# Adapter rows loaded during stage 0, staged tiles asked for one weight group later, and the adapter sums' mask moved to ScalarE

## The reference, cut to what is computed

```python
# layer 0: a dense layer plus a signed one, scaled per batch item
x = x + (x @ W.T + b + (x @ (2 * mask[b] - 1)) * coeff[b])
# layer 1: gated feed-forward (F = 2752), each product with a rank-16 adapter chosen per batch item
def lora_add(base, inp, A, B):
    t = einsum('bri,bni->bnr', A[idx], inp)
    return base + einsum('bor,bnr->bno', B[idx], t) * 0.5
gate = lora_add(x @ W_gate.T, x, A_gate, B_gate)
up   = lora_add(x @ W_up.T,   x, A_up,   B_up)
act  = silu(gate) * up
x = x + lora_add(act @ W_down.T, act, A_down, B_down)
```

## Time and profile before

| | us |
|---|---|
| median of three runs (1623.53 to 1625.01) | 1624.55 |
| the profiled execution, its own time | 1624.44 |
| its span, first to last instruction | 1622.4 |
| TensorE busy | 1562.2 |
| VectorE busy | 1223.7 |
| ScalarE busy | 795.9 |
| POOL busy | 355.1 |
| mean granted TensorE clock | 0.993 |

### The profile page before, as it was taken

How to read it: one execution, slowest core, us unless ns; L and a number is a source line. 1 busy time by engine, 2 the same in 40 slices (tenths; PEclk the granted TensorE clock), 3 DMA queues, 4 the chain that set the end, 5 groups by cost and what they waited for, 6 DMA issues and landing times. The chain is left out here.

```text
span 1622.4 us, 23032 instructions
## 1 busy us (share of the span) xinstructions
PE 1562.2 (96%) x7508; PEld 1309.9 (81%) x7508; DVE 1223.7 (75%) x2150; ACT 795.9 (49%) x1478; POOL 355.1 (22%) x677
## 2 busy tenths in 40 slices
PE   6999978999999999999999979999999999999999
PEld 6999956888888888878887757888888888778887
DVE  7998858666667667688887797666666666788886
ACT  7998835444444444443333454444444444433332
POOL 0100021222222222253420012212222222442100
PEclk9999989999999999999999999999999999999999
DMA  8979653444444444698592723444444444996653
GB/s 327 354 285 332 230 166 91 147 147 153 153 153 153 152 136 138 215 358 271 184 372 93 256 73 118 152 148 143 136 145 153 153 153 142 333 346 207 228 198 120
DMA packets 135046, 316.85 MB, mean 195 GB/s; under 512 B 19856, under 2 KB 43536, under 8 KB 134928
## 3 DMA queue, kind: packets, MB, share of 16 engines
q0 software_dynamic: 56608, 175.81, 32.8%
q1 hardware_dynamic: 73712, 131.18, 24.1%
q10 hardware_dynamic: 4608, 8.39, 1.4%
HBM read 225.13 MB, written 90.18 MB: 194 GB/s over the span
## 5 line engine op out<-in xcount | busy, mean ns | idle before, releaser
L1435 PE MATMUL ps<-op_b,hi 128*128 128x512 f32 x1616 | 501.0, 391 | 4.2 <-ACT ps L748 3.3
L1067 DVE TENSOR_TENSOR lo<-raw,hi 128x512 fp32r<-128x512 f32 (+2 forms) x640 | 333.3, 530 | 134.6 <-ACT hi L748 132.7
L748 ACT ACTIVATE hi<-raw 128x512 fp32r<-128x512 f32 (+1 forms) x592 | 304.4, 518 | 224.0 <-PE ps L1435 176.5
L1435 PEld LDWEIGHTS ps<-op_b,hi 128*128 128x128 f32 x1616 | 304.7, 189 | 70.5 <-ACT ps L748 4.1
L1435 PE MATMUL ps<-op_b,lo 128*128 128x512 f32 x808 | 316.9, 392 | 0.0
L1435 PE MATMUL ps<-op_d,hi 128*128 128x512 f32 x800 | 250.4, 394 | 14.4 <-DVE acc L1070 12.3
L1431 PE MATMUL ps<-op_b,hi 128*128 128x512 f32 x816 | 254.6, 393 | 0.0
L625 POOL DMA_DIRECT2D operand_scratch<-ot x140 | 75.6, 540 | 641.8 <-DVE ot L1067 606.3
L1070 DVE TENSOR_TENSOR acc<-acc,ps 128x512 f32<-128x512 f32 x248 | 169.8, 685 | 55.1 <-PE ps L1435 48.8
L1435 PEld LDWEIGHTS ps<-op_d,hi 128*128 128x128 f32 x800 | 148.2, 189 | 52.2 <-DVE acc L1070 19.6
L1431 PEld LDWEIGHTS ps<-op_b,hi 128*128 128x128 f32 x816 | 154.3, 189 | 33.8
(11 more groups left out here) (122 smaller groups left out, 2216.7 us busy)
## 6 DMA issues: line engine op xcount, KB each, us to landing
operand_scratch<-ot POOLq DMA_DIRECT2D x140, 512.0 KB, 3.9
op_d<-operand_scratch POOLq DMA_DIRECT2D x140, 512.0 KB, 10.4
raw<-in_wgu SPq DMA_DIRECT2D x168, 256.0 KB, 4.2
m_raw<-in_mask SPq DMA_DIRECT2D x64, 512.0 KB, 5.7
raw<-in_wd SPq DMA_DIRECT2D x160, 128.0 KB, 3.9
b_in<-in_b_gu POOLq DMA_DIRECT2D x264, 32.0 KB, 2.3
w_in<-in_w SPq DMA_DIRECT2D x16, 512.0 KB, 5.4
x_scratch<-x_out POOLq DMA_DIRECT2D x32, 256.0 KB, 5.0
```

Source lines behind the costliest of these rows:

```text
L748: return nc.scalar.activation(o, i, ACT.Copy)
L1067: return nc.vector.tensor_tensor(o, a, b, ALU.subtract)
L1435: return mm(dst, weight, v, start=False, stop=stop, skip_group_check=True)
```

## The change

Five edits.

1. POOL loads the adapter matrix of block 0 after the store of x1 tile 20 and not behind the whole of stage 0. To have free memory for it, `ad_in` moves behind `b_in1`, and the filler `pad_lw` goes; `a_in` then lies where the input buffer `x_in` of stage 0 was, and POOL waits for the last use of that.
2. `lora_a` makes two tiles of `lw` in one instruction on each engine. The first two such pairs move from event h(0,1) to h(0,0), ahead of the four b12 operands.
3. SP issues the early tiles of block 1 one weight group later: tiles 0 and 1 after the second group of the last segment, 2 and 3 after the third, 4 and 5 after the fourth, 6 and 7 after the four weights of block 1's first pair.
4. In `form_t_gu` the two mask multiplications (64x256 each) and the first high part (32x512, twice) go from VectorE to ScalarE. VectorE keeps the addition and the two low parts.
5. The second call of `form_t_gu` in a block, t(1), moves from behind p1's `evict` to the event ta(1,7) ahead of it; the four t3 operands move from h(1,7) to the event g p1.

```diff
+A_GU_AT = 20
...
-    return {("h", 0, 0): forms("b12", 0, 1, 2, 3),
-            ("h", 0, 1): a_part((0, 0), (0, 1), (0, 2), (0, 3)),
+    return {("h", 0, 0): a_part(0, 0, 2) + forms("b12", 0, 1, 2, 3),
             ("h", 0, 3): forms("b22", 0, 1, 2, 3),
-            ("ta", 0, 1): a_part((0, 4), (0, 5)) + [("make", 0)],
+            ("ta", 0, 1): a_part(0, 4) + [("make", 0)],
...
-            ("h", 1, 7): forms("t3", 0, 1, 2, 3),
-            ("g", 1, "p1"): [("t", 1)],
+            ("ta", 1, 7): [("t", 1)],
+            ("g", 1, "p1"): forms("t3", 0, 1, 2, 3),
...
                 for u in PLAIN:
                     weight_dma(("g", s, 0), WEIGHT[u])
+                if s:
+                    for i in (2 * HP - 2, 2 * HP - 1):
+                        early_dma(s, i)
...
-                        if seg == SEGS - 1 and s < BLOCKS - 1:
-                            for i in (2 * hp, 2 * hp + 1):
+                        if seg == SEGS - 1 and hp and s < BLOCKS - 1:
+                            for i in (2 * hp - 2, 2 * hp - 1):
                                 early_dma(s + 1, i)
...
                 pool.dma_start(x1_d[s, o, h, :, :], x1_out[:, q % X1_RING, :]).then_inc(x1_stored[q % X1_RING], 16)
-
-            adapter = adapters(0)
+                if q == A_GU_AT:
+                    adapter = adapters(0)
+                    pool.wait_ge(xl_ready, BLOCKS * 2 * HT)
+                    load_a_gu(adapter)
+
             pool.wait_ge(pe_done, last_s)
...
-            load_a_gu(adapter)
             load_b_gu(adapter, 0)
...
                 copy(u2[0:2 * R2, :], ps[6 + half][2 * R2:4 * R2, :]).then_inc(ta_low, 1)
+                act.wait_ge(ta_sum, 2 * s + half + 1)
+                for b in range(2):
+                    cols = slice(b * S, (b + 1) * S)
+                    nc.scalar.activation(u2[0:2 * R2, cols], g2[0:2 * R2, cols], ACT.Copy, scale=own_sb[:, b:b + 1]
+                                         ).then_inc(ta_own, 1)
                 act.wait_ge(ta_own, 2 * (2 * s + half + 1))
                 for dst, r in ((t_gate[half], 0), (t_up[half], R2)):
-                    copy(dst[R2:2 * R2, :], g2[r:r + R2, :]).then_inc(t_hi, 1)
+                    copy(dst[0:R2, :], u2[r:r + R2, :])
+                    copy(dst[R2:2 * R2, :], u2[r:r + R2, :]).then_inc(t_hi, 1)
...
                 add(g2[0:2 * R2, :], ps[6 + half][0:2 * R2, :], u2[0:2 * R2, :]).then_inc(ta_sum, 1)
-                dve.wait_ge(ta_sum, m + 1)
-                for b in range(2):
-                    cols = slice(b * S, (b + 1) * S)
-                    nc.vector.tensor_scalar(g2[0:2 * R2, cols], g2[0:2 * R2, cols], own_sb[:, b:b + 1], None, ALU.mult
-                                            ).then_inc(ta_own, 1)
-                dve.wait_ge(ta_own, 2 * (m + 1))
                 for i, (dst, r) in enumerate(((t_gate[half], 0), (t_up[half], R2))):
-                    nc.vector.tensor_copy(dst[0:R2, :], g2[r:r + R2, :]).then_inc(t_top, 1)
-
-                    dve.wait_ge(t_top, 2 * m + i + 1) if r == 0 else dve.wait_ge(t_hi, 2 * m + 2)
-                    sub(dst[2 * R2:3 * R2, :], g2[r:r + R2, :], dst[r:r + R2, :]).then_inc(t_ready, 1)
+                    dve.wait_ge(t_hi, 2 * m + i + 1)
+                    sub(dst[2 * R2:3 * R2, :], u2[r:r + R2, :], dst[r:r + R2, :]).then_inc(t_ready, 1)
```

More of the change, by code:

```diff
@@ L60, in first_tile_steps, with a_part @@
 def first_tile_steps():
-    def a_part(*uses):
-        return [("lw", *use) for use in uses]
+    def a_part(half, *firsts):
+        return [("lw", half, o) for o in firsts]
     def forms(name, *ks):
         return [("form", name, k) for k in ks]
-    return {("h", 0, 0): forms("b12", 0, 1, 2, 3),
-            ("h", 0, 1): a_part((0, 0), (0, 1), (0, 2), (0, 3)),
+    return {("h", 0, 0): a_part(0, 0, 2) + forms("b12", 0, 1, 2, 3),
             ("h", 0, 3): forms("b22", 0, 1, 2, 3),
-            ("ta", 0, 1): a_part((0, 4), (0, 5)) + [("make", 0)],
-            ("ta", 0, 3): a_part((0, 6), (0, 7)) + [("make", 1)] + forms("t1", 0),
-            ("ta", 0, 5): a_part((1, 0), (1, 1)) + [("make", 2)] + forms("t1", 1),
-            ("ta", 0, 7): a_part((1, 2), (1, 3)) + [("lora_b",), ("t", 0), ("make", 3)] + forms("t1", 2, 3),
+            ("ta", 0, 1): a_part(0, 4) + [("make", 0)],
+            ("ta", 0, 3): a_part(0, 6) + [("make", 1)] + forms("t1", 0),
+            ("ta", 0, 5): a_part(1, 0) + [("make", 2)] + forms("t1", 1),
+            ("ta", 0, 7): a_part(1, 2) + [("lora_b",), ("t", 0), ("make", 3)] + forms("t1", 2, 3),
             ("h", 1, 1): forms("t2", 0, 1),
-            ("ta", 1, 1): a_part((1, 4), (1, 5)) + forms("t2", 2, 3),
-            ("ta", 1, 3): a_part((1, 6), (1, 7)),
+            ("ta", 1, 1): a_part(1, 4) + forms("t2", 2, 3),
+            ("ta", 1, 3): a_part(1, 6),
             ("r", 0): [("result", 0)],
@@ L806, in lora_a @@
                     act.wait_ge(a_loaded, 16 * 4 * (s + 1))
-                    dst = lw[:, r, 0:2 * R2].rearrange("p (m r) -> p m r", r=RANK)
-                    copy(dst, a_in[:, 4 * half:4 * half + 4, o * RANK:(o + 1) * RANK]).then_inc(lw_h, 1)
+                    dst = lw[:, r:r + 2, 0:2 * R2].rearrange("p o (m r) -> p o m r", r=RANK)
+                    src = a_in[:, 4 * half:4 * half + 4, o * RANK:(o + 2) * RANK].rearrange("p m (o r) -> p o m r", r=RANK)
+                    copy(dst, src).then_inc(lw_h, 1)
                 else:
@@ L1122, in lora_a @@
                     _, s, half, o = key
-                    tile = lw[:, r, :].rearrange("p (q m r) -> p q m r", q=2, r=RANK)
-                    src = a_in[:, 4 * half:4 * half + 4, o * RANK:(o + 1) * RANK]
-                    sub(tile[:, 1, :, :], src, tile[:, 0, :, :]).then_inc(lw_l, 1)
+                    tile = lw[:, r:r + 2, :].rearrange("p o (q m r) -> p o q m r", q=2, r=RANK)
+                    src = a_in[:, 4 * half:4 * half + 4, o * RANK:(o + 2) * RANK].rearrange("p m (o r) -> p o m r", r=RANK)
+                    sub(tile[:, :, 1, :, :], src, tile[:, :, 0, :, :]).then_inc(lw_l, 1)
                 else:
```

13 lines of the change are left out of this document (6 added, 7 removed).

## The result

The changed kernel has a median of 1612.62 us over four runs (1612.1 to 1614.97), the kernel before 1624.78 us over four runs (1623.53 to 1625.47). The ratio is 0.9932, with a 95% interval from 0.9919 to 0.9945: faster by 0.7%. The prediction was 1613.8 us, range 1607.5 to 1619.5.

A forecast was written before the change was run, and what follows sets the result against it. TensorE was taken as the bound, busy 1562.2 of 1622.4 us, so only waits and low clock could be won. From 1624.44: block 0 entry -5.5 + 0.8, block 1 entry +2.6 + 0.4, transition -8.9, giving 1613.8 us, range 1607.5 to 1619.5.

The forecast's parts named there:

- step a): Block 0's entry: `fx` tiles land at 0.87 us a tile, and the last b22 operand is formed at 215.9.
- b): Entries: pairing saves 0.7 us up to the addition of t(0); in block 0 `b_in` puts that addition at 226.5.
- Step d): Block 0's entry: `lw` pairs for ta(1,4) at 236.5 and the next at 241.9, TensorE waiting for both as before.
- none for `t_up`: Sign to look for after the change: no TensorE wait for `t_up`, beside a 6 to 7 us wait for p1's copy.
- Edit 4's chain: Addition to last low part, crossing to ScalarE: 4.9 us against 3.66, 1.25 more a chain, bounds 3.7 and 5.5.
- Rival 1: ScalarE's part of the chain overlaps fully, four chains cost 3.7 each: 5 us less, 1608.8 us; chance 0.12.
- the rows can't tell the two engines apart: Edit 4: profile rows can't show whether ScalarE or VectorE suits the multiplications; the sum already has a 1.25 us loss a chain.
- the copy's new place: Block 1's entry: p1's copy behind t(1)'s chain in ScalarE's queue adds 1.6 us.
- rival 3: Transition: SP's new order does nothing, since ring cells hold the weights; 1622.7 us, chance 0.05.
- rival 4: Transition: block 1's first weights hold SP to the segment's end (912), tiles 6 and 7 come late; 1627.8 us, chance 0.03.
- rival 2: Entries: after the 6.6 us wait p6, r(1) and p3 run at 1.2 GHz, 2.8 more each; 1619.4 us, chance 0.13.
- the clock term: Entries: low clock after the wait for p1's copy adds 0.8 us in block 0 and 0.4 in block 1.

The follow-up runs named there:

- e9: e8 with the first twelve `b_in` loads of block 0 asked for in stage 0, after x1 tile 28; 1601.55 us, ratio 0.9867 to the kernel before.
- e1: Edits 1 and 2 alone on the kernel before; 1613.82 us, ratio 0.9934.
- e5: Edits 1, 2 and 3 alone on the kernel before, edits 4 and 5 left out; 1606.26 us, ratio 0.9890.
- The square: Four kernels with edits 1 to 3, with or without edits 4 and 5; entries (block 0 / block 1) from 55.60 / 52.54 to 59.63 / 56.19 us.
- e4: The changed kernel without edit 5, t(1) again behind p1's copy; 1612.36 us, ratio 0.9926 to the kernel before.
- e3: The changed kernel without edit 4, mask and first high parts on VectorE again; 1608.47 us, ratio 0.9897 to the kernel before.
- e6: The changed kernel with p1's copy ahead of t(1), t(1) still ahead of the t3 operands; 1614.67 us, ratio 0.9943 to the kernel before.
- e2: Edit 3 alone on the kernel before; 1616.69 us, ratio 0.9952.
- e8: e5 with `t_neg` made behind the gate's silu and not ahead of p5's copy; 1604.06 us, ratio 0.9873 to the kernel before.
- e11: e9 without the pairing of `lw` tiles; 1604.99 us, ratio 0.9882 to the kernel before.
- e10: The changed kernel without the pairing of `lw` tiles; 1614.15 us, ratio 0.9944 to the kernel before.

## Why the prediction was right, step by step

**Block 0's entry (forecast -4.7, measured -5.1).** The last b22 operand of step a) was formed at 216.75, 0.85 us later than forecast (215.9). From b) on the dates came out within 0.4 us: addition of t(0) 226.23 (226.5 forecast), end of chain 231.17 (231.4), `lw` for ta(1,4) awaited until 236.27 (236.5), addition of t(1) 249.72 (250.1), p6 255.97 (256.3), `p5c` 259.67 (259.6), release of the adapter matmul 264.91 (264.8). What bounded the first date was named right, `b_in`, but by little: ScalarE waits 2.59 us for it, VectorE only 0.39, and without it (e9) VectorE's own queue gives 20.06 us after the first matmul in place of 20.95. Two things were read wrong, without harm to the sum. Step d) has TensorE wait for both pairs of `lw` tiles "as before", but the timeline of before has no wait near 249.55 in block 0, and the changed kernel has none for the second pair either. And "none for `t_up`" held for r(1) only: in front of r(0) TensorE waits 2.87 us. The dates were those of VectorE's queue, which did set them. The net of -5.1 hides two large terms that e1, e5 and the changed kernel separate: -9.1 for the early load (64.75 to 55.60) and +4.0 for edits 4 and 5.

**Edit 4's chain (forecast 4.9 for 3.66, measured 4.94).** Right in the sum and in its parts: two multiplications 0.91 (0.77 forecast), four copies 2.57 (2.6), last low part 0.68. Rival 1, a full overlap, is out: copies of 32x512 in a row start 0.65 us apart, not 0.52. The square gives 2.6 us for two chains in block 1, 2 x 1.28. The Trainium skill, ScalarE: Activation LUTs, Rules for kernel authors, puts multiplications on VectorE; the runs agree, and here the prediction missed rows that it could have had. VectorE's two 64x256 multiplications in before take 0.61 us together, ScalarE's 0.91, and VectorE's high part 0.42 where ScalarE's copy takes 0.63. The timeline of VectorE of before, just behind the addition in the earlier trace rows:

```profile
236.09 0.61 DVE L1204 TENSOR_SCALAR g<-g,own_sb 64x256 f32<-64x256 f32 x2
236.73 0.42 DVE L1208 CAST t_gate<-g 32x512 fp32r<-32x512 f32 x1
```

So "the rows can't tell the two engines apart" was wrong. Of the 1.28 us, 0.30 are the multiplications. The other 0.98 stand between the end of the multiplications and the last low part: four copies in ScalarE's queue, 0.65 us apart, where VectorE had two casts and a subtraction (2.60 against 1.62 us). How much of that is the slower copy and how much the one queue, no run here tells apart.

**Edit 5 (forecast wait 6.6 us, measured 6.37 and 6.34).** Right in the mechanism: p1's copy is delayed by ScalarE's queue, and what releases p3's adapter matmul is `b_w`. The wait it took over, for `t_up` in front of r(1), is not in the earlier trace rows; the timeline of TensorE of before has it:

```profile
264.53 0.47 PE L1435 MATMUL ps<-t_gate,b_w 96*128 96x512 f32 x1 [2.40 <-DVE t_up L1067]
```

With the 1.63 for p1's copy, a further 0.49 for `p5c` and 0.44 for `b_w`, TensorE waited 4.96 us between p5 and that matmul before, and waits 7.56 now. Edit 5's price on the path is 1.0 to 1.1 us with edit 4 in place (e4) and 1.3 to 1.4 without (e3 against e5). The prediction names +1.6 for the copy's new place, but its terms for block 1 (-0.7, two chains at +1.25, +1.6) add up to +3.4, not to the +2.6 of its sum; the sum from the dates (22.9 - 20.75 = 2.15, of which 1.25 is the chain) holds only 0.9 for edit 5, close to what came out. e6 takes the wait away and gains 1.0 and 0.4 us.

**Block 1's entry (forecast +2.6 and +0.4 clock, measured +3.7).** Three terms were mis-sized. The pairing's -0.7 in b) measured nothing: the addition of t(0) comes 17.47 us after the first matmul, 17.55 before. The row at 915.86 shows why: ScalarE waits until the second of the two ring slots is free, 7.90 us after the first matmul, while the unpaired copy of before could start for the first slot alone, at 7.45 (929.74). And from the end of p1's copy to `p5c` it takes 3.76 us (255.91 to 259.67), not 3.3, since VectorE's low part of the last t3 ends 1.15 us after ScalarE is ready. Together these are 1.2 us. The third is the clock, which cost nothing on this path (below), so that the +3.0 came closer than its parts. By the square edits 4 and 5 account for all of it (3.65 of 3.73).

**The transition (forecast 29.0, measured 28.92).** Right; e2 shows that SP's order does it alone, which rules out rival 3. The dates of the tiles were right too. They are counted from the second group's start, 884.40 in the kernel before and 879.04 here. From that start tile 4 was forecast to go at 4.6 us and tile 5 at 8.6, tiles 6 and 7 at 14.0 and 18.1; SP takes up tiles 4 and 5 at 4.6 and is through with them at 9.1 us (888.1), and does the same with 6 and 7 at 14.2 and 18.6 (897.7). Block 1's first weights were issued by 891.1, 17 us ahead of the segment's end, which rules out rival 4. The stall's price depends on the clock: 7.7 us in e1, where the waits left it at 1.00, 9.0 in before's profile with a mean of 0.95.

**Clock (forecast +0.8 and +0.4, measured nothing in the entries).** p6 runs at the lower level, as forecast, and is at full speed again for its last matmuls (4.61 us from its start to r(1), 5.2 forecast); rival 2 is out. Behind it TensorE still waits 1.19 and 0.97 us for `b_w`, so that the slow p6 is hidden and the 0.8 and 0.4 were not paid. In block 0 the dates without the clock term give -5.5 and -5.1 was measured; the -4.7 with it was met by two errors of opposite sign, which is luck. The busy time of the changed kernel behind four resumptions, after waits of 2.19, 6.37, 6.34 and 0.97 us (clock is the last column but two):

```profile
236.27:241.00 4.73, 4.73 (x15) 3.80 (x16) 4.59 (x8) 2.04 (x5) 0.00 (x0) 0.68 0.29 100
255.97:259.90 3.93, 3.93 (x10) 3.11 (x11) 3.10 (x5) 2.78 (x6) 0.00 (x0) 0.52 0.39 127
955.16:959.00 3.84, 3.84 (x9) 3.06 (x10) 3.10 (x5) 2.69 (x6) 0.00 (x0) 0.50 0.34 118
964.15:970.00 5.85, 5.85 (x26) 4.83 (x27) 3.25 (x5) 2.33 (x5) 0.56 (x1) 1.00 0.07 25
```

In the first of the four the clock was low before the wait of 2.19 us: from 232.59 on two matmuls take 1.05 us in place of 0.62, behind the 2.87 us wait for `t_up`.

What the prediction left out is the other side of it: in before, the matmuls behind 974.75 were slow too.

```profile
974.75:980.00 5.25, 5.25 (x16) 4.20 (x17) 3.25 (x5) 1.73 (x3) 0.56 (x1) 0.67 0.00 0
```

16 matmuls in 5.25 us, where 23 fit at 0.228: 1.6 us that the changed kernel does not pay there (0.97 us of wait, clock 1.00 behind it). It is the -1.5 of the last stretch. That the span came out 1.5 us lower than the sum has its reason here. It is luck and no part of the forecast: e2, with before's order of events in block 1, had its low clock just ahead of that place (two matmuls at 964.37 take 1.05 us), where its wait for `b_w` shrank to 0.49 us, and none behind it. So before need not pay it each time. The other differences cancel (-0.4 in block 0, -0.3 in stage 0, +0.7 in block 1).

**Stage 0.** No wait between 130 and 160 us, as forecast, with 0.92 DMA share.

## What to carry to other kernels

A change that bundles edits can be a clear gain and still hold losses: edits 1 and 2 together and edit 3 are worth 9 us each, edits 4 and 5 cost 7.7 together, and leaving the two out is faster than the whole. Work moved to an idle engine can lengthen the path although both engines have time to spare: count the chain, not the busy time. And a long wait of the bounding engine is priced by what is released behind it, not by its length: a wait of 6.4 us was taken away here for 1.0 and 0.4. A forecast of a bundle can also be right in its total with terms in it that were never paid (pairing, clock); experiments on single edits show it.

## What the runs showed of the hardware

**The clock after a wait of 2.3 us is not always the same.** All kernels wait 2.28 or 2.29 us for `acc` at one place of block 1's down part. Stretches of 100 us around it, in the changed kernel and in e6:

```profile
1350.00:1450.00 100.00, 95.79 (x417) 76.83 (x416) 77.85 (x162) 42.72 (x94) 40.41 (x75) 1.00 0.92 303
```

```profile
1350.00:1450.00 100.00, 95.88 (x412) 77.10 (x411) 77.04 (x161) 42.40 (x94) 40.50 (x75) 0.98 0.92 303
```

The row behind the wait, in e6 (its two matmuls take 1.14 us, 0.73 at full speed):

```profile
1396.46 1.14 PE L1437 MATMUL ps<-op_d,hi 128*128 128x512 f32 x2 [2.28 <-DVE acc L1080]
```

Of the 13 profiles (before, the changed kernel twice, ten others) seven show a clock of 1.00 in such a stretch and six 0.98; in the six the next wait comes 16.3 to 16.6 us after this one, in the others 15.2, so 1.2 to 1.4 us are lost. Block 0's down part waits as long at the same place, and there three of the 13 (e2, e8, e11) have the low clock and lose 1.3 us: nine cases of 26. The waits of 5.1 to 6.5 us for p1's copy were followed by the low clock in all eight entries that have them (the changed kernel twice, e3, e10): the first row behind each has 1.22 us for two matmuls. The Trainium skill, TensorE: Matmul & The Clock Gate, HAM oscillation, says that idle gaps throttle TensorE again and that each resumption then pays. The traces agree for the waits of over 5 us; after 2.3 us at these two places nine of 26 paid. For a comparison of kernels it means an uncertainty of up to about 1.4 us at each such place that has nothing to do with the edit, so that landmarks tell small edits apart and medians do not.

**A low clock in the shadow of another wait is free, as far as the shadow goes.** In the changed kernel p6 took 4.61 us in block 0, some 1.9 more than its 12 matmuls need at 0.228, and TensorE still waited 1.19 us for `b_w` behind it. In e8 p3 ran slow in block 0 and came to its adapter matmul at 260.72, when `b_w` had been ready since 260.24: there about 0.4 us of the low clock showed.
